# Recurrent layer in three passes of split operands, and the context quantised one layer later

## The reference, cut to what matters

```python
# layer 1, recurrent (RG-LRU), width 640
left  = gelu(x @ Wl + bl)
conv  = causal_conv4(x @ Wr + br) + conv_b         # four taps, per channel
r, i  = sigmoid(conv @ Wa + ba), sigmoid(conv @ Wi + bi)
log_a = -8 * softplus(-lam) * r
a     = exp(log_a)
drive = sqrt(max(1 - exp(2 * log_a), 1e-12)) * (i * conv)
h_t   = a_t * h_(t-1) + drive_t                     # scan over 512 steps
x = layernorm(x + (left * h) @ Wo + bo)
# layer 2, experts by token id: 4 experts, expert = id // 6250
g = x @ W[e].T ; y = (silu(g) * g) @ W[e].T         # W is the context itself
x = layernorm(x + y)
# layer 5: the context in fp8 with one scale
scale = 448 / max(|ctx|); q = fp8(clip(ctx * scale, -448, 448)) / scale
```

## Time and profile before

| | |
|---|---|
| time, median of 3 runs | 2483.17 us (2480.9 to 2489.24) |
| profiled execution, its own time | 2481.16 us |
| profiled execution, span from first to last instruction | 2479.4 us |
| TensorE busy | 2218.7 us, 89% |
| VectorE busy | 1401.2 us, 57% |
| ScalarE busy | 675.1 us, 27% |
| GpSimd busy | 695.5 us, 28% |
| recurrent layer | 0 to about 391 us |
| token-id layer | about 391 to 539 us |

### The profile page before, as it was taken

The page is one execution under the profiler, slowest core; times in us unless marked ns, Lnnn a source line. Parts: engine busy times, 40 slices in busy tenths (PEclk is TensorE's granted clock), DMA queues, the critical chain, the costliest instruction groups (busy, mean ns, idle before and its releaser), DMA issues. The chain is left out here.

```text
span 2479.4 us, 29975 instructions
## 1 busy us (share of the span) xinstructions
PE 2218.7 (89%) x10235; PEld 1054.4 (43%) x10238; DVE 1401.2 (57%) x3204; ACT 675.1 (27%) x1186; POOL 695.5 (28%) x1018
## 2 busy tenths in 40 slices
PE   9999997979999999889999987478888888799993
PEld 4444444865444443444444443233333333345441
DVE  6999985647311215466676674945657564522224
ACT  2222322321012220333434332523232222002223
POOL 2210002326423221323333433011113131125552
PEclk9999998989999999999999998689999999999997
DMA  7332102234057775264333330310000000065444
GB/s 277 136 102 84 54 16 67 82 141 173 10 172 250 246 229 169 76 141 85 78 84 78 85 66 1 110 71 2 1 19 1 18 27 18 18 200 88 86 86 150
DMA packets 101700, 235.45 MB, mean 95 GB/s; under 512 B 18918, under 2 KB 42646, under 8 KB 94398
## 3 DMA queue, kind: packets, MB, share of 16 engines
q1 hardware_dynamic: 79006, 191.83, 24.7%
q0 software_dynamic: 22560, 41.87, 7.9%
HBM read 174.69 MB, written 63.53 MB: 96 GB/s over the span
## 5 line engine op out<-in xcount | busy, mean ns | idle before, releaser
L1913 DVE CUSTOM_DVE_ANT_0 D_ps<-D_ps,D_mask 128x256 f32<-128x256 f32 (+1 forms) x512 | 186.8, 420 | 70.2 <-PE D_ps L1810 69.2
L1662 POOL TENSOR_SCALAR_AFFINE_SELECT D_probs<-D_probs 128x256 f32<-128x256 f32 x256 | 106.1, 420 | 288.6 <-ACT D_probs L1720 288.4
L1720 ACT ACTIVATE D_probs<-D_ps 128x512 f32<-128x512 f32 (+1 forms) x256 | 125.3, 543 | 165.4 <-PE D_ps L1832 165.2
L2913 DVE TENSOR_REDUCE F_neg_max<-F_ps 128x4 f32<-128x2048 f32 (+1 forms) x64 | 93.9, 1489 | 107.9 <-PE F_ps L2811 101.8
L3355 PE MATMUL G_ps<-G_gate_up,G_xgT 128*128 x304 | 138.6, 599 | 0.3 <-DVE G_xgT L3446 0.3
L2663 ACT ACTIVATE F_probs<-F_ps 128x1536 f32<-128x1536 f32 (+1 forms) x48 | 76.4, 1591 | 186.0 <-PE F_ps L2827 186.0
L1223 PE MATMUL C_ps<-C_down_shared,C_hs 128*128 128x512 f32 x256 | 114.0, 594 | 3.2 <-DVE C_hs L1390 2.1
L1211 PE MATMUL C_ps<-C_xT,C_gate_shared 128*128 128x512 f32 x256 | 115.4, 593 | 0.5 <-ACT C_xT L1086 0.5
L1211 PE MATMUL C_ps<-C_xT,C_up_shared 128*128 128x512 f32 x256 | 115.1, 592 | 0.0
L1810 PE MATMUL D_ps<-D_k_stack,D_q_stack 96*128 96x256 bf16 (+1 forms) x512 | 92.2, 265 | 8.7 <-DVE D_maxima L1913 7.3
L1060 POOL DMA_INDIRECT expert_sums<-C_y,C_of_slot x32 | 50.2, 1570 | 173.5 <-ACT C_y L1127 116.5
(11 more groups left out here) (508 smaller groups left out, 4582.9 us busy)
## 6 DMA issues: line engine op xcount, KB each, us to landing
C_ring<-moe_experts_dram SPq DMA_DIRECT2D x32, 1536.0 KB, 7.1
qk_parts<-D_parts SPq DMA_DIRECT2D x32, 384.0 KB, 2.6
B_w<-ctx_dram SPq DMA_DIRECT2D x8, 1024.0 KB, 6.0
expert_sums<-A_cq SPq DMA_DIRECT2D x1, 8192.0 KB, 28.2
C_ring<-expert_sums SPq DMA_DIRECT2D x5, 1536.0 KB, 10.0
D_q_stack<-qk_parts SPq DMA_DIRECT2D x16, 384.0 KB, 4.9
D_k_stack<-qk_parts SPq DMA_DIRECT2D x16, 384.0 KB, 7.9
B_w<-ctxT_dram SPq DMA_DIRECT2D x1, 4096.0 KB, 15.1
```

The costliest lines, as they stand in the source:

```text
L1662: last = nc.gpsimd.affine_select(now[:, :, 0:P], now[:, :, 0:P], [[0, 2], [1, P]], ALU.is_ge, 0.0, base=0, channel_multiplier=-1)
L1720: nc.scalar.activation(probs[at % 2][:, 2 * pair:2 * pair + 2, 0:w], ps[:, 4 + unit % 3, :].rearrange("p (h q) -> p h q", h=2)[:, :, 0:w], ...
L1913: last = nc.vector.tensor_tensor_reduce(now, now, mask[:, first:256], 1.0, -3e38, ALU.add, ALU.max, maxima[n % 2][:, head, t:t + 1])
L2913: last = nc.vector.tensor_reduce(neg_max[n % 2][:, :, t], ps[:, 0:GROUP, at:at + w], AX_X, ALU.max, negate=True)
```

## The change

In the recurrent layer Wl, Wr, Wa, Wi, x turned and u (the convolution's output) are split into high and low parts in float32r. All right, left and gate products use three passes, but for the right and left branch of batch 0; the output product stays float32. ScalarE copies the high parts and VectorE subtracts for the low parts, in place where it can. The fourth tap of the convolution moves to ScalarE. ScalarE takes an Exp beside the Tanh, in two groups of decay tiles (0 to 2, then 3 and 4), and VectorE needs four operations and no reciprocal for decay and variance; the square roots now come before the input gates. The bias is added by VectorE, rows are normalised in place, and the next rows' load waits for their store. The expert weights are split at the end of this stage. The context leaves this stage; in the token-id layer its maximum is taken in tiles 0 to 3, and its quantisation, 5 operations per batch, is dealt over tiles 5 to 18. There the normalisation moves from VectorE to ScalarE, with a shift that GpSimd multiplies out; five tiles are in flight instead of four.

```diff
@@ recurrent layer, SyncE @@
             sp.dma_start(wa[:], d["L0_attn_Wa"].rearrange("(k p) n -> p k n", p=P)).then_inc(wa_in, 16)
+            sp.dma_start(wi[:], d["L0_attn_Wi"].rearrange("(k p) n -> p k n", p=P)).then_inc(wi_in, 16)
             sp.dma_start(xrow[:], d["x"][0:S, :].rearrange("(t p) n -> p t n", p=P)).then_inc(xr_in, 16)
-            sp.dma_start(wi[:], d["L0_attn_Wi"].rearrange("(k p) n -> p k n", p=P)).then_inc(wi_in, 16)
...
-            store_c(0)
-            load_c(B + 2)
-            store_c(1)
-            load_c(B + 3)
+            load_xT(2)
             store_rows(0)
+            sp.wait_ge(out_done, 16)
             load_rows(1)
-            load_xT(2)
             sp.wait_ge(scattered, 16 * T)
             sp.dma_start(who[:], table.rearrange("(p t) o -> p (t o)", p=P)).then_inc(who_in, 16)
-            store_c(2)
-            store_c(3)
-            sp.dma_start(w_b[:], d["ctxT"].rearrange("e (k p) f -> p e k f", p=P)).then_inc(w_b_in, 16)
+            load_xT(3)
             store_rows(1)
+            sp.wait_ge(out_done, 16 * 2)
             load_rows(2)
-            load_xT(3)
             sp.wait_ge(tile_done, L_done(B - 1, KH - 1))
-            load_rows(B - 1)
+            sp.dma_start(xrow_last[:], d["x"][bass.ds((B - 1) * S, S), :].rearrange("(t p) n -> p t n", p=P)).then_inc(xr_last_in, 16)
+            sp.dma_start(w_b, d["ctxT"].rearrange("e (k p) f -> p e k f", p=P)).then_inc(w_b_in, 16)
@@ recurrent layer, ScalarE @@
+            def high_x(b):
+                act.wait_ge(x_in, b * 16)
+                nc.scalar.copy(x_hi, xT[:]).then_inc(x_hi_ready, 1)
...
+            def last_taps(row):
+                for m in range(KH):
+                    act.wait_ge(r_ready, row * KH + (m + 1))
+                    if row:
+                        act.wait_ge(scanned, (row - 1) * KH + (m + 1))
+                    nc.scalar.activation(u[:, m, :], rin[:, m, 3:], ACT.Identity, bias=col(vec, "conv_b", m),
+                                         scale=col(vec, "w3", m)).then_inc(tap_ready, 1)
...
+            def high_u(b, m):
+                act.wait_ge(conv_done, b * KH + m + 1)
+                nc.scalar.copy(u_hi[:, m, :], u[:, m, :]).then_inc(u_hi_ready, 1)
+
+            def decays(b, first, after):
+                for m in range(first, after):
                     act.wait_ge(tile_done, A_done(b, m))
                     nc.scalar.activation(a[:, m, :], ps[:, (A_at(b) + m) % 8, :], ACT.Sigmoid,
                                          bias=col(vec, "ba", m)).then_inc(act_took, 1)
...
+                for m in range(first, after):
                     act.wait_ge(act_took, A_took(b, m))
+                    nc.scalar.activation(beta[:, m, :], a[:, m, :], ACT.Exp, scale=minus_twice_rate[:, m:m + 1])
                     nc.scalar.activation(a[:, m, :], a[:, m, :], ACT.Tanh, scale=rate[:, m:m + 1]).then_inc(a_ready, 1)
...
+            act.wait_ge(wa_in, 16)
+            nc.scalar.copy(flat(wa_hi), flat(wa)).then_inc(wa_hi_ready, 1)
+            right(0)
+            last_taps(0)
+            left_and_high_u(0)
+            act.wait_ge(wi_in, 16)
+            nc.scalar.copy(flat(wi_hi), flat(wi[:])).then_inc(wi_hi_ready, 1)
+            nc.scalar.copy(flat(wr_hi), flat(wr)).then_inc(wr_hi_ready, 1)
+            decays(0, 0, 3)
+            decays(0, 3, KH)
+            high_x(1)
+            act.wait_ge(wl_in, 16)
+            nc.scalar.copy(flat(wl_hi), flat(wl[:])).then_inc(wl_hi_ready, 1)
+            roots(0)
+            input_gates(0)
+            right(1)
+            for b in range(1, B):
+                last_taps(b)
+                left_and_high_u(b)
+                if b < B - 1:
+                    high_x(b + 1)
+                decays(b, 0, 3)
+                decays(b, 3, KH)
+                roots(b)
+                input_gates(b)
+                if b < B - 1:
                     right(b + 1)
-
-            right(0)
-            for b in range(B - 1):
-                one_pass(b, True)
-            one_pass(B - 1, False)
+            act.wait_ge(w_b_in, 16)
+            for e in range(EXPERTS_B):
+                nc.scalar.copy(flat(w_b_hi[:, e]), flat(w_b[:, e])).then_inc(w_b_hi_ready, 1)
@@ recurrent layer, TensorE @@
+                for k in range(chunks):
+                    if first_of is not None:
+                        pe.wait_ge(u_hi_ready, first_of * KH + k + 1)
+                    nc.tensor.matmul(out, w_hi[:, k, now], x_hi[:, k, :], start=(k == 0), stop=False)
+                for k in range(chunks):
+                    nc.tensor.matmul(out, w_lo[:, k, now], x_hi[:, k, :], start=False, stop=False)
+                for k in range(chunks):
+                    if first_of is not None:
+                        pe.wait_ge(u_lo_ready, first_of * KH + k + 1)
+                    last = nc.tensor.matmul(out, w_hi[:, k, now], x_lo[:, k, :], start=False, stop=(k == chunks - 1))
@@ recurrent layer, VectorE @@
+            def variances(b):
+                for m in range(KH):
+                    dve.wait_ge(a_ready, b * KH + (m + 1))
+                    steps.after(nc.vector.tensor_scalar(inverse[:], beta[:, m, :], 0.5, 0.5, ALU.mult, ALU.add))
+                    steps.after(nc.vector.tensor_tensor(beta[:, m, :], a[:, m, :], inverse[:], ALU.mult))
+                    steps.after(nc.vector.tensor_scalar(a[:, m, :], beta[:, m, :], -2.0, 1.0, ALU.mult, ALU.add))
+                    last = nc.vector.scalar_tensor_tensor(out=beta[:, m, :], in0=beta[:, m, :], scalar=0.25e-12, in1=inverse[:],
+                                                          op0=ALU.max, op1=ALU.mult)
...
             recurrence(0)
+            steps.restart()
             convolve(1)
+            low_x(2)
+            add_bias(0)
+            normed_rows(0)
+            variances(1)
+            recurrence(1)
...
+            recurrence(3)
+            low_w_b()
+            normed_rows(2)
+            normed_rows(3)
@@ token-id layer @@
-        E, AHEAD = EXPERTS_B, 4
+        E, AHEAD = EXPERTS_B, 5
...
+        OPS, FIRST_QUANT, LAST_QUANT = 5, B + 1, TILES_B
+        def parts_of_c(n):
+            return [divmod(i, OPS) for i in range(OPS * B) if FIRST_QUANT + i * (LAST_QUANT - FIRST_QUANT) // (OPS * B) == n]
...
                 nc.gpsimd.tensor_tensor(rstd[:, n:n + 1], mv[:, n, 1:2], power[:], ALU.pow).then_inc(rstd_ready, 1)
+                pool.wait_ge(rstd_ready, n + 1)
+                nc.gpsimd.tensor_tensor(shift[:, n:n + 1], mv[:, n, 0:1], rstd[:, n:n + 1], ALU.mult).then_inc(shift_ready, 1)
...
+            def normalise(n):
+                act.wait_ge(shift_ready, n + 1)
+                if n >= AHEAD:
+                    act.wait_ge(stored[n % AHEAD], 16 * (n // AHEAD))
+                nc.scalar.activation(y[n % AHEAD][:], res[n % AHEAD][:], ACT.Identity, bias=shift[:, n:n + 1],
+                                     scale=rstd[:, n:n + 1]).then_inc(y_ready, 1)
...
                 if n >= 1:
                     high_h(n - 1)
+                if n >= 2:
+                    normalise(n - 2)
                 if n < TILES_B:
                     squares(n)
+            normalise(TILES_B - 1)
...
+            def turn_amax():
+                pe.wait_ge(c_amax_ready, 1)
+                pe.wait_ge(sum_ready, B - 2)
+                nc.tensor.transpose(ps[:, 6 + (B - 1) % 2, 0:P], c_amax_wide[:], ident[:]).then_inc(c_amax_turned, 1)
...
+            def quantise_c(b, part):
+                now = c[:, b]
+                if part == 0:
+                    steps.after(nc.vector.tensor_scalar(now, now, c_scale[:], FP8_MAX, ALU.mult, ALU.min))
+                elif part == 1:
+                    steps.after(nc.vector.tensor_scalar(big.bitcast(I32)[:], now.bitcast(I32), 0x7F800000, None, ALU.bitwise_and))
+                elif part == 2:
+                    steps.after(nc.vector.tensor_scalar(big[:], big[:], 2.0 ** -6, ROUND, ALU.max, ALU.mult))
+                elif part == 3:
+                    steps.after(nc.vector.scalar_tensor_tensor(out=now, in0=now, scalar=-FP8_MAX, in1=big[:], op0=ALU.max, op1=ALU.add))
+                else:
...
+                    nc.vector.tensor_tensor(cq[:], now, big[:], ALU.subtract).then_inc(c_ready, 1)
...
                 if n >= 1:
                     low_h(n - 1)
-                if n >= 2:
-                    normalise(n - 2)
+                if n == B:
+                    scales_of_c()
                 hidden(n)
+                if n < B:
+                    see_c(n)
+                for b, part in parts_of_c(n):
+                    quantise_c(b, part)
                 if n >= 1:
                     moments(n - 1)
```

More of the change, by code:

```diff
@@ L371, in _, with product @@
+            for e in range(EXPERTS_B):
+                nc.scalar.copy(flat(w_b_hi[:, e]), flat(w_b[:, e])).then_inc(w_b_hi_ready, 1)
         @block.tensor
         def _(pe):
-            def product(tile, w, m, moving, chunks):
```

(43 more changed lines are left out.)

371 lines of the change are left out of this document (186 added, 185 removed).

## The result

| | before | after |
|---|---|---|
| median (range) of 4 runs each, side by side | 2486.07 us (2480.9 to 2489.24) | 2452.90 us (2445.6 to 2457.85) |
| profiled execution: its time / span | 2481.16 / 2479.4 us | 2453.74 / 2452.0 us |

A forecast was written before the change was run, and what follows sets the result against it. TensorE was taken to bound the recurrent layer, a three-engine chain the changed token-id layer. Terms of -46.8 and +27.1 us summed to -19.7, taking the median from 2483.2 to 2463.5, stated as 2462 us; range 2438 to 2478.

The forecast's parts named there:

- the forecast's own 2452 to 2472: Whole kernel: the central case around 2462 us, given 65%.
- 320 matmuls to 960, -50.7: Recurrent layer, TensorE: 320 float32 matmuls at 0.8585 us become 960 float32r ones at 0.2333 us, 50.7 us less.
- The rival of 0.2147 us: Recurrent layer: the narrow matmuls take 0.2147 us each, a further -17.9 us, time 2444 us; chance 10%.
- No other engine late in the middle batches: Recurrent layer: VectorE needs 57 us against TensorE's 80.2 per batch, with 14 to 15 us to spare.
- Last batch +1.2, tail +2.7: Recurrent layer's end: last taps and splits come 1.2 us late; the end after the last matmul grows by 2.7 us.
- Start of the token-id layer, -2.7: Token-id layer's start: weight splits leave, two gathers remain; 2.7 us less, between 0 and 5.
- The loop over three engines, +27.7: Token-id layer: a chain over ScalarE, VectorE and GpSimd paces the tiles, 138.0 us from squares(1) to squares(18) against 110.3.
- the rival without a loop: Token-id layer: the loop does not bind, the layer costs about +3 us and the time is 2438 us; chance 12%.
- the chain without its piece: Token-id layer: time from one tile's squares to the next without the context work between, summed to 5.77 us.
- End of the token-id layer, +2.1: Token-id layer's tail: the last piece delays the low half of h by 1.2 us, the longer last chain adds 0.9.
- The clock in the token-id layer: Token-id layer: a rival where the granted clock falls as TensorE waits, +27 us, time 2489 us; chance 6%.

The follow-up runs named there:

- the kernel with two passes: The changed kernel with the pass of the low weights left out of the recurrent layer's products; its last normalisation starts at 301.28 us, 38.4 us earlier.
- the first group: Changed kernel again (2482.3 us), with ScalarE's squares ahead of normalisation (2462.1 us), with context work on 8 of 2048 columns, with normalisation back on VectorE; kernel before 2509.4 us.

## Why the prediction was right

The time was forecast at 2462 and is 2452.9, inside the stated range and at the very edge of the forecast's own 2452 to 2472; in the profiled pair the gain is 27.4 us where 19.7 was summed. Step by step:

- **320 matmuls to 960, -50.7.** Shown: 0.2333 us each, 51.8 us back with native matmuls, of which 0.8 lie ahead of the changed products. The rival of 0.2147 us is refuted here: a float32r matmul with a weight load of its own takes 233 ns in the rows. The Trainium skill ("TensorE: Matmul & The Clock Gate", section "Wait — 56ns, not 53.3ns?") has 215.7 ns for back-to-back matmuls of 512 columns at the full clock. That section does not name float32r, and the trace does not agree with it for these matmuls.
- **No other engine late in the middle batches.** Shown, with more room than I had given (at least 21.2 us, not 14): I measured the spare time at the end of a chain and left out the idle stretches inside it.
- **Last batch +1.2, tail +2.7.** Measured 0.7 and 3.1 (last matmul to the end of the last normalisation, 6.2 us against 3.1). The tail is VectorE's, which is without idle time from 297 to 327 us. With these terms the stage would be at -46.9; the other 1.4 us are first gates that start 0.6 us earlier than before (41.15, 41.73) and batches of 79.86 us where 80.2 were summed.
- **Start of the token-id layer, -2.7.** Mis-sized, -5.6, outside the bound of 5 that I gave: the last normalisation to the first product takes 10.87 us instead of 15.48. From there to the first Tanh it is 4.15 instead of 5.15, and that is the clock: granted 0.50 up to 352 us, so only the first group of four is slow (351.10, then 352.97, 354.12), where two and a half were before (403.98, 405.84, 407.54).
- **The loop over three engines, +27.7.** The mechanism was right (the rival without a loop would have left the spacing near 6.5), down to the pattern of spacings: predicted 8.1, 8.2, 8.6, 6.5 from tile 1, measured 7.48, 7.47, 9.38, 6.50; 10.4 at tiles 7 and 14, measured 9.97 and 9.94. The term that was mis-sized is the chain without its piece: 5.3 us, not 5.77. GpSimd's added product takes 0.18 us where I took the 0.50 next to the power's 0.56, and VectorE's operations overlap by 0.08 where I had added whole durations. Some 0.47 us on 16 tiles are 7.5; 0.8 of it went at tile 3 and 1.0 in the short pieces, which took 1.40, 1.27 and 1.33 us on average where the earlier trace rows had 1.29, 1.23 and 1.23. At tile 3 TensorE's turn of the maxima, placed ahead of the first product of tile 4, waits for the last maximum, which I had not put on the path, and behind this pause the granted clock was 0.50 from 380.8 to 384.1 us. So the product took 4.45 us (380.28 to 384.73) where the next tile's took 2.89, and it, not the chain, released the Tanh:

```profile
380.08 0.33 PE L921 MATMUL B_ps<-ident,B_c_amax_wide 128*128 128x128 f32 x1 [1.99 <-DVE B_c_amax_wide L989]
...
384.93 0.60 ACT L840 ACTIVATE B_th<-B_ps 128x512 f32<-128x512 f32 x1 [1.33 <-PE B_ps L908]
```

- **End of the token-id layer, +2.1.** Mis-sized, 0.9: TensorE, with nothing else left to do, turned the last hidden tile 1.85 us after its Tanh (494.91) instead of 2.60 (527.37 against 524.77). I had let it start as before.
- **The clock in the token-id layer.** The mean stayed at 0.98 while TensorE was busy for 89%: the rival did not come at its price of 27 us. The clock fell only for short stretches, behind tile 3 and at the end of the layer, and where I had priced nothing, in the untouched layer behind.

The sum was closer than its terms by luck: the loop and the start were 8.4 us too dear, the clock of the MoE layer, which no term had, took 7.0 back, and the later layers gave 3.6 by chance. By these numbers the kernel without the fall would be near 2446 (an estimate, 2452.9 less 7.0), below the forecast's own 2452 though still in the stated range.

## What to carry to other kernels

When an operation moves to an in-order engine, ask what its wait closes: here the work moved was 0.8 us a tile and its place in front of the next tile's first operation cost 18 us in the layer; behind it, the same move cost nothing. Long filler work is free only where no chain runs through its engine at that point. The spare time of a stage is what stands idle at the end of its chain plus every idle stretch inside, and the first and last rounds of a loop have less of it than the middle ones. Where it runs out, TensorE can lose more than the wait: behind the pauses of 6.14 and 6.33 us in the kernel with two passes its granted clock was 0.50.

## What was not expected of the hardware

The clock at the start of the MoE layer, above: 6 to 7 us that come and go, mostly with changes in the layer ahead of it. And a pause in the same layer, in the four profiles of the first group and in none of the ten others. VectorE in the changed kernel there, in order of time, with the idle time ahead of it:

```profile
586.52 0.42 DVE L1451 TENSOR_TENSOR C_biased<-C_ps,C_bias 128x256 f32<-128x256 f32 x1 [26.54 <-remote]
```

VectorE's pause at this place was 26.5, 25.9, 14.9 and 25.7 us in the four, ScalarE stood idle for 29 to 33 us where it is 21.3 elsewhere, and TensorE was held up with them, while GpSimd went on with its scatters until 582.6. The layer is some 20 to 24 us longer for it, about what every kernel of that group had more, so the kernel before very likely had it too, though it was not profiled there. Its cause is open. Comparisons of totals within that group are uncertain by the few us by which it varied.
